# Where eight class rows run in a vision tower: a step of their own after the images, or beside images 1 and 2

## The reference, cut to what matters

```
x = _layernorm(x, gamma, beta)
x = x + gelu(x @ w1.T + b1) @ w2.T + b2          # 256 -> 1024 -> 256
h = h + _layernorm(x, gamma, beta)
m = _layernorm(h)
logits = silu(m @ rw1 + rb1) @ rw2 + rb2         # the router: 256 -> 1024 -> 8
k_logits, k_index = top_k(logits, 2); k_prob = softmax(k_logits)
for e in range(8):
    we = sum(where(k_index == e, k_prob, 0))
    out += we[:, None] * (silu(m @ w1[e] + b1[e]) @ w2[e] + b2[e])
return h + out
```

## Time and profile before

| | |
|---|---|
| median of 3 runs | 787.42 us (785.85 to 788.01) |
| the profiled execution's own time | 786.85 us |
| its span | 785.1 us |
| busy: PE / PEld / DVE / ACT / POOL | 710.4 / 624.2 / 330.0 / 296.2 / 289.0 us |
| PE busy, share of the span | 90% |
| chain that ended last | PE 72%, DVE 10%, issue 6% |

### The profile page before, as it was taken

How to read it: one execution, slowest core, us unless ns; L and a number is a source line. 1 busy time by engine, 2 the same in 40 slices (tenths; PEclk the granted TensorE clock), 3 DMA queues, 4 the chain that set the end, 5 groups by cost and what they waited for, 6 DMA issues and landing times.

```text
span 785.1 us, 15021 instructions
## 1 busy us (share of the span) xinstructions
PE 710.4 (90%) x4633; PEld 624.2 (80%) x4634; DVE 330.0 (42%) x1003; ACT 296.2 (38%) x761; POOL 289.0 (37%) x324
## 2 busy tenths in 40 slices
PE   0887999999999999999999829999999999999994
PEld 0766889988887878778876728988999899999893
DVE  5576757654424234443443461323233232333320
ACT  0433655665433335444451303333233332333321
POOL 6022866676652243445432220222232232222222
PEclk9968989999689999999998859999999999999997
DMA  9515999400000990110011324121121122112210
GB/s 222 181 23 113 287 285 288 112 0 1 1 1 1 365 333 15 41 42 28 20 35 42 136 83 143 35 34 32 34 34 34 30 34 39 24 33 34 41 20 1
DMA packets 53219, 63.92 MB, mean 81 GB/s; under 512 B 6348, under 2 KB 48768, under 8 KB 53008
## 3 DMA queue, kind: packets, MB, share of 16 engines
q1 hardware_dynamic: 43616, 53.76, 23.7%
q0 software_dynamic: 8112, 9.04, 6.8%
q10 hardware_dynamic: 1456, 0.68, 0.4%
HBM read 31.01 MB, written 31.38 MB: 79 GB/s over the span
## 4 chain that ended last, share of the span: by engine, by line
PE 72%; DVE 10%; issue 6%; DMA 3%; ACT 3%; POOL 2%; SPq 1%; POOLq 0%; DVEq 0%; ACTq 0%
PE bank L1538 68%; DMA arena<-in_L_tok_Wa 2%; POOL small L502 1%; DVE small L481 1%; ACT dense L1514 1%; DVE arena L941 1%; DMA h<-arena 1%; PE bank L1991 1%; PE bank L1855 1%; PE bank L1716 1%; POOL arena L679 1%; DVE arena L494 1%; PE bank L1570 1%; ACT arena L1436 1%; DVE dense L1173 1%
## 5 line engine op out<-in xcount | busy, mean ns | idle before, releaser
L1538 PE MATMUL bank<-arena,dense 128*128 128x256 f32 (+3 forms) x1472 | 317.6, 386 | 14.7 <-ACT dense L1514 6.0
L1538 PEld LDWEIGHTS bank<-arena,dense 128*128 128x128 f32 (+1 forms) x1472 | 256.1, 194 | 58.1 <-issue 20.5
L1514 ACT ACTIVATE dense<-bank,small 128x128 f32<-128x128 f32 x320 | 91.3, 369 | 196.8 <-PE bank L1538 196.8
L766 POOL DMA_INDIRECT out_tokens<-dense,slot_ids x40 | 77.6, 1940 | 237.7 <-DVE dense L1291 206.2
L1538 PEld LDWEIGHTS bank<-dense 128*128 128x128 f32 x1280 | 150.4, 193 | 2.0
L1538 PE MATMUL bank<-dense 128*128 128x128 f32 x1280 | 150.5, 276 | 0.0
L1538 PE MATMUL bank<-dense,arena 128*128 128x256 f32 (+2 forms) x656 | 107.7, 358 | 1.2 <-ACT arena L1378 0.7
L1538 PEld LDWEIGHTS bank<-dense,arena 128*128 128x128 f32 (+2 forms) x656 | 85.4, 193 | 19.2 <-issue 6.8
L679 POOL TENSOR_TENSOR arena<-arena 128x512 f32<-128x512 f32 x64 | 80.3, 1278 | 40.3 <-ACT arena L1398 40.3
L1538 PE MATMUL bank<-arena 128*128 128x34 f32 (+7 forms) x756 | 82.7, 304 | 1.3 <-issue 0.5
L1538 PEld LDWEIGHTS bank<-arena 128*128 128x128 f32 (+4 forms) x756 | 75.4, 179 | 9.5 <-issue 5.4
(11 more groups left out here) (213 smaller groups left out, 545.1 us busy)
## 6 DMA issues: line engine op xcount, KB each, us to landing
routed_rows<-x SPq DMA_DIRECT2D x8, 2385.0 KB, 26.1
arena<-in_L_ffn_w SPq DMA_DIRECT2D x16, 1024.0 KB
dense<-routed_rows SPq DMA_DIRECT2D x40, 132.5 KB
arena<-in_x SPq DMA_DIRECT2D x4, 512.0 KB, 7.0
arena<-in_L_attn_w SPq DMA_DIRECT2D x2, 1024.0 KB
out_tokens<-h SPq DMA_DIRECT2D x8, 256.0 KB
h<-arena SPq DMA_DIRECT2D x13, 128.0 KB
dense<-in_L_ffn_rw SPq DMA_DIRECT2D x1, 1024.0 KB, 9.5
```

Of the source, the lines that this page charges most:

```text
L766: pool.indirect_dma_start(out=sums[:, :], out_offset=bass.IndirectOffsetOnAxis(ap=slot_ids[par][:, 0:1], axis=0), in_=y[par], in_offset=No ...
L1514: act.activation(hT[par][:, k, :], psUP[par][c][:, P * m:P * m + P], ACT.Silu, bias=b1now[par][:, k:k + 1]).then_inc(hT_sb, 1)
L1538: return pe.matmul(out, lhsT, rhs, start=start, stop=stop, **kw)
```

## The change

Group 8 leaves the tail. Its work gets semaphores of its own (`c_...`), its own small buffers, and runs inside steps 1 and 2:

- Step 1: after image 2 is turned, the class rows are turned between the two tiles of `mlp_out(1)`, and their first MLP matrix (`class_hidden(w1T, ...)`) follows them.
- Step 2: `class_mlp_out` stands behind `router_out(0)`. It waits for the class rows' Gelu and for `h1_ready` to reach 2, that is the end of image 1's `finish_rows` up to its sum. Their router matrix, router output, sum and ranks stand between and behind the tiles of `mlp_out(2)`.
- DVE in step 2: `finish_rows(1)`, `finish_rows(8)`, `choose(0)`, `norm_x1(3)`, `settle(0)`, `choose(8)`, `settle(8)`; only then `finish_rows(2)` of step 3. POOL ends step 2 with `scatter(0)` and `scatter(8)` (two indirect DMAs of 8 rows).
- Step 7: `mlp_out(7)` moves ahead of the other image's router matrix (that of image 6), with `ranks(5)` between its tiles. In the tail `xm_T(7)` moves ahead of `router_sum(6)`, and `ranks(6)` stands between two halves of image 7's router matrix.

The core of the diff, PE first:

```diff
+            def class_turn(ready, src, turned_):
+                pe.wait_ge(ready, 1)
+                for k in range(KD):
+                    ins = pe.transpose(psC[:, k * B:(k + 1) * B], src[:, k * P:k * P + P], ident[0:B, 0:B])
+            def class_hidden(w, src, turned_, done):
+                pe.wait_ge(turned_, 1)
+                for m in range(KH):
+                    for k in range(KD):
+                        ins = mm(psF[0][:, m * B:(m + 1) * B], w[:, k, P * m:P * m + P], src[:, k, :],
+                                 k == 0, k == KD - 1)
+            def class_mlp_out():
+                pe.wait_ge(c_gelu_sb, 1)
+                pe.wait_ge(h1_ready, 2)
+                for k in range(KH):
+                    ins = mm(psO[0][0:B, 0:D], c_gT[:, k, :], w2T[:, k, :], k == 0, k == KH - 1)
+            def class_router_out():
+                pe.wait_ge(c_silu_sb, 1)
+                for k in range(KH):
+                    p0 = GROUP * (k % 4)
+                    ins = mm(psLT[p0:p0 + GROUP, 0:B], rw2[:, k, :], c_rT[:, k, :], k < 4, k >= 4)
+            def class_router_sum():
+                pe.wait_ge(c_lgT_sb, 1)
+                mm(psLG[0:B, 0:E], c_lgT[:, :], sel).then_inc(c_lg_ps, 1)
...
             def routing_step(g, par):
                 if not peeled or g >= 2:
+                    router_out(g - 2, par, router_use - 8)
+                if peeled and g == 2:
+                    class_mlp_out()
+                pe.wait_ge(x1T_sb, g + 1)
+                hidden(mlp_use, w1T, x1T[par], IMG)
...
+                xm_T(g - 1, 1 - par)
+                if peeled and g == B - 1:
+                    mlp_out(g, par, 0, mlp_use)
+                    ranks(g - 2)
+                    mlp_out(g, par, 1, mlp_use)
+                pe.wait_ge(xmT_sb, g)
+                hidden(router_use, rw1, xmT[1 - par], IMG)
+                if peeled and g == 2:
+                    class_turn(c_xm, c_pay[:, 0, :], c_xmT_ps)
+                if not peeled or g + 1 < B:
                     x1_T(g + 1, 1 - par)
-                if not peeled or g >= 2:
+                if not peeled or 2 <= g < B - 1:
                     ranks(g - 2)
-                if not peeled or g <= B:
-                    for j in range(1 if peeled and g == B else T):
+                if peeled and g == 1:
+                    mlp_out(g, par, 0, mlp_use)
+                    class_turn(c_xh, cx[0:B, 2, :], c_x1T_ps)
+                    mlp_out(g, par, 1, mlp_use)
+                    pe.wait_ge(m_sb, router_use + 4)
+                    class_hidden(w1T, c_x1T, c_x1T_sb, c_gelu_ps)
+                elif peeled and g == 2:
+                    pe.wait_ge(m_sb, router_use + 3)
+                    class_hidden(rw1, c_xmT, c_xmT_sb, c_silu_ps)
+                    mlp_out(g, par, 0, mlp_use)
+                    class_router_out()
+                    mlp_out(g, par, 1, mlp_use, range(0, 2))
+                    class_router_sum()
+                    mlp_out(g, par, 1, mlp_use, range(2, KH))
+                    ranks(B)
+                elif not peeled or g < B - 1:
+                    for j in range(T):
                         mlp_out(g, par, j, mlp_use)
...
-            mlp_use, use, last_use = 8 * B - 4, 8 * B, 8 * B + 4
+            use = 8 * B - 4
             router_out(B - 2, 0, 8 * (B - 1))
-            pe.wait_ge(x1T_sb, B + 1)
-            hidden(mlp_use, w1T, x1T[0], B)
-            mlp_out(B, 0, 0, mlp_use)
+            xm_T(B - 1, 1)
             router_sum(B - 2, 0)
-            xm_T(B - 1, 1)
             pe.wait_ge(xmT_sb, B)
-            hidden(use, rw1, xmT[1], IMG)
+            hidden(use, rw1, xmT[1], IMG, range(0, 2))
             ranks(B - 2)
-            xm_T(B, 0)
+            hidden(use, rw1, xmT[1], IMG, range(2, 4))
             router_out(B - 1, 1, use)
-            pe.wait_ge(xmT_sb, B + 1)
-            hidden(last_use, rw1, xmT[0], B)
             router_sum(B - 1, 1)
             ranks(B - 1)
-            router_out(B, 0, last_use)
-            router_sum(B, 0)
-            ranks(B)
```

DVE, ACT and POOL follow the same order. The parts that the prediction speaks of:

```diff
             # DVE routing_step
+                if peeled and g == 2:
+                    finish_rows(B, 0)
                 if not peeled or g >= 2:
                     choose(g - 2, par)
-                if not peeled or g + 1 <= B:
+                if not peeled or g + 1 < B:
                     norm_x1(g + 1, 1 - par)
                 if peeled and g == 1:
+                    norm_class()
                 if not peeled or g >= 2:
                     settle(g - 2, par)
+                if peeled and g == 2:
+                    choose(B, 0)
+                    settle(B, 0)
...
             finish_rows(B - 1, 1)
-            finish_rows(B, 0)
...
-            choose(B, 0)
-            settle(B, 0)
             # ACT
+            def class_hidden(done, func, bias, dst, read):
+                act.wait_ge(done, 1)
+                for m in range(KH):
+                    ins = act.activation(dst[:, m, :], psF[0][:, m * B:(m + 1) * B], func, bias=bias[:, m:m + 1])
             # POOL routing_step
                 if not peeled or g >= 2:
                     scatter(g - 2, par)
+                if peeled and g == 2:
+                    scatter(B, 0)
             # SP
-            sp.wait_ge(mlp_ps, T * B + 1)
+            sp.wait_ge(mlp_ps, T * B)
             sp.wait_ge(experts_loaded, LOW_LOADED)
             load_first(E - 2)
```

More of the change, by code:

```diff
@@ L574, in _ @@
                 store_h1(2 * it + 1, 1)
-            sp.wait_ge(h1_ready, B + 1)
+            sp.wait_ge(c_h1, 1)
             sp.dma_start(sums.rearrange("(b q) n -> b q n", b=B)[:, 0, :],
@@ L748, in _ @@
             routing_step(B - 1, 1)
[L750 to L754, removed]
+            root(pool, link, P, T, m_var, m_root, 2 * B - 1)
+            root(pool, link, P, T, m_var, m_root, 2 * B)
+            for g in (B - 2, B - 1):
                 scatter(g, g % 2)
@@ L1187, in finish_rows @@
                     dve.wait_ge(done, (g - par) * (16 * T))
-                after(dve, xmT_ps, g - 1)
-                normalize(dve, link, hrow, lambda j: rows[0:n, j, 0:D], n, tiles, m_var, m_root, 2 * g + 2
-                          ).then_inc(xm_ready, 1)
+                if not tail:
+                    after(dve, xmT_ps, g - 1)
+                normalize(dve, link, hrow, lambda j: rows[0:n, j, 0:D], n, tiles, var, root_, asked + 1
+                          ).then_inc(c_xm if tail else xm_ready, 1)
             dve.tensor_reduce(sel, ident.rearrange("p (g s) -> p s g", g=4)[:, 0:E, :], AX_X, ALU.add
@@ L1454, in _, with logits_T, gate_halves @@
                      ).then_inc(cattT_sb, 1)
-            def logits_T(g, n):
+            def logits_T(g):
                 act.wait_ge(lgT_ps, g + 1)
                 after(act, lg_ps, g)
-                act.copy(lgT[:, 0:n], psLT[:, 0:n]).then_inc(lgT_sb, 1)
-            def gate_halves(g, tiles, rows):
-                act.wait_ge(lg_gap, g + 1)
+                act.copy(lgT[:, :], psLT[:, 0:IMG]).then_inc(lgT_sb, 1)
+            def gate_halves(g):
+                tail = isinstance(g, int) and g == B
+                rows, tiles = (B, 1) if tail else (P, T)
+                gapped, count = of(g, lg_gap, c_gap)
+                act.wait_ge(gapped, count)
                 act.activation(half[0:rows, 0:tiles, :], gap[0:rows, 0:tiles, :], ACT.Tanh, scale=0.5
-                               ).then_inc(lg_half, 1)
+                               ).then_inc(c_half if tail else lg_half, 1)
             def routing_step(g, par):
@@ L1488, in _ @@
             routing_step(B - 1, 1)
-            logits_T(B - 2, IMG)
-            hidden(B, 8 * B - 4, ACT.Gelu, b1T, gT, B)
+            logits_T(B - 2)
             xm_T(B - 1, 1)
-            hidden(B - 1, 8 * B, ACT.Silu, rb1T, rT, IMG)
-            gate_halves(B - 2, T, P)
-            xm_T(B, 0)
-            logits_T(B - 1, IMG)
-            hidden(B, 8 * B + 4, ACT.Silu, rb1T, rT, B)
-            gate_halves(B - 1, T, P)
-            logits_T(B, B)
-            gate_halves(B, 1, B)
+            hidden(B - 1, 8 * B - 4, ACT.Silu, rb1T, rT, IMG, range(0, 2))
+            gate_halves(B - 2)
+            hidden(B - 1, 8 * B - 4, ACT.Silu, rb1T, rT, IMG, range(2, 4))
+            logits_T(B - 1)
+            gate_halves(B - 1)
             def rows_T(i, par):
@@ L1846, in x1_T @@
                 ins.then_inc(x1T_ps, 1)
             def xm_T(g, par):
-                tail = isinstance(g, int) and g == B
-                n, tiles = (B, 1) if tail else (P, T)
                 pe.wait_ge(xm_ready, g + 1)
-                after(pe, x1T_sb, g + 2 if not isinstance(g, int) or g + 2 <= B else B + 1)
-                for j in range(tiles):
+                after(pe, x1T_sb, g + 2 if not isinstance(g, int) or g + 2 <= B else B)
+                for j in range(T):
                     for k in range(KD):
-                        ins = pe.transpose(psT[:, k * IMG + j * P:k * IMG + j * P + n],
```

(3 more changed lines are left out.)

247 lines of the change are left out of this document (153 added, 94 removed).

## The result

| | before | after |
|---|---|---|
| median | 786.63 us (785.48 to 788.01, 4 runs) | 801.60 us (800.92 to 803.52, 4 runs) |
| ratio | | 1.0193 (95% interval 1.0167 to 1.0220) |
| profiled execution, own time / span | 786.85 / 785.1 us | 801.68 / 799.9 us |
| PE / DVE / ACT / POOL busy | 710.4 / 330.0 / 296.2 / 289.0 us | 709.3 / 330.2 / 293.5 / 289.3 us |
| span's start to step 1 | 242.4 us | 241.3 us |

The account below looks back on a forecast made before the run. PE was taken to bound the kernel where full, and the chain through the other engines where PE stands still. Terms -17.2 + 15.5 + 6.4 = +4.7 us on 786.85 gave 791.8 us, range 784.5 to 796.5.

Parts of the forecast that it names:

- What the tail gives back: Router output 5 to first expert tile: 56.7 us instead of 73.9, so 17.2 us gained.
- POOL's collision in step 7: Group 5's scatter on POOL holds the first root of finish_rows(7) back by 2.1 us.
- The landing of the last scatter: In the tail, ahead of the experts: time for the scatter to land, taken as 1.5 us, bounded by 0 and 3.
- Steps 1 to 3 without the clock: Class rows on a full PE, with late DVE in step 3: 3.85 + 8.15 + 3.5 = 15.5 us paid.
- The clock, 6.4 for four places: Clock falls at four stretches in steps 1 to 3 and the tail, 85% at 1.9 us each: 6.4 us.
- The fourth: Tail stretch from Silu wait and router output 6 through a 1.6 us stall to ACT wait: 5.1 us, a likely clock fall.
- A: Step 1's class hidden matrix, router output and stall: a 5.3 us stretch where the clock would likely fall.
- B: Step 2's class turn, turn, ranks and class hidden matrix: a 5.1 us stretch where the clock would likely fall.
- the forecast's own -1.7: Whole kernel without clock falls: 15.5 us paid in steps 1 to 3 against 17.2 gained in the tail, a small gain.
- Engine lateness does not show: Rival: no POOL collision in step 7 or DVE lateness in step 3, so 783.5 us; chance 0.16.
- The tail's work does not shrink as said: Rival: scatter's landing or last expert weight loads take 3 us more in the tail; chance 0.05.

Follow-up runs that it names:

- e1: The changed kernel with the Tanh of group 5's gates moved ahead of the Silu of image 6's router matrix in ACT's list; 792.1 us.
- e6: e5 with image 5's scatter behind both roots of finish_rows(7) in POOL's list and a buffer of their own for image 7's rows; 783.0 us.
- e3: e1 with the class rows' router output, sum and ranks put earlier among the MLP tiles of image 2; 789.9 us.
- e4: e3 with the class rows' thin router-matrix records mixed in eights between the four units of image 1's router matrix; 790.5 us.
- e5: e4 with POOL's two class scatters moved from step 2 to the tail, behind the scatter of image 6; 786.0 us.
- e7: e6 with the class rows' MLP matrix mixed into image 1's second tile, a bank part for their second matrix and their turn moved; 782.4 us.

## Why the prediction was wrong, step by step

- **The step that failed** is in "What the tail gives back": "Settle of group 5 starts at 13.8, lasts 1.94". It started at 13.5 (427.07 less 413.55) and lasted 12.6, to 439.7. The 1.94 is settle's length when the Tanh is there. The diff of PE's order was read closely, and for DVE and POOL I asked what stands ahead of each wait; for ACT I did not. Row 411.35 of the earlier trace rows was used only for the Silu's length. e1 shows the size: 9.5 us of the 9.8 that the forecast missed by, and in the tail 11.0 of the 12.6 between 56.7 and 69.3; the other 1.6 is a clock fall that the forecast had in another term.
- POOL's collision in step 7: right in place and size, once the Tanh is in place. 2.02 us of PE wait in e1 (1.6 forecast), and image 7 was turned 28.0 us after router output 5, as forecast; e6 takes the wait away.
- Tail without the Tanh: 56.7 and one fall forecast, 58.3 in e1. The landing of the last scatter, set at 1.5 within 0 to 3, is about 2.5: in the changed kernel POOL's last scatter ends at 477.7 and the row loads go out at 480.2.

```profile
480.23 1.48 SPq L637 DMA_DIRECT2D dense<-routed_rows  x2
```

From there to the first expert tile go 2.6 us (to 482.82), where the forecast took 3.39, counted from the tables. The two errors nearly cancel, 10.8 from places to experts against 10.5 forecast. That part of the agreement is luck.
- Steps 1 to 3 without the clock, 15.5: 20.7 measured, less the three falls of 1.4, 1.8 and 2.3 read from the rows above, leaves 15.2. PE's wait in step 3 was 3.24 us, 2.85 more than before against 2.9 forecast. e3 takes 1.8 of it away (settle earlier), and the class scatters on POOL were worth 1.0 from e4 to e5, against 0.7 forecast. Two sums of the forecast are 0.05 off (the terms of step 2 add up to 8.2, and 8.96 should read 8.9); nothing hangs on it.
- The clock, 6.4 for four places: all four fell, at 1.4, 1.8, 2.3 and about 2.0, together 7.5. The fourth stood behind a wait of 12.69 us here and not of 1.6; the stretch that the forecast had in mind is in e1, where the half matrix lost 1.7. That busy thin stretches keep the clock did not hold for A and B: both are busy, and where the same records stood mixed with wide ones (e4 for B, e7 for A) these falls were gone. In e7 the mixing was not the only edit. The sentence of the Trainium skill ("TensorE: Matmul & The Clock Gate", Part 1: The HAM clock gate), that the gate goes by how busy the PE has been recently, does not cover this by PE's busy share as the profile counts it: in the changed kernel PE was busy 3.82 us on end and the clock was at 1.2 GHz behind it.
- That the sum's sign came from the clock was wrong for the changed kernel: by the forecast's own -1.7 and the Tanh's 9.5 it would have been slower without any fall. For e1 it fits: 5.0 us over the kernel before, with falls of about 7 in its rows. No run shows e1 without the falls and otherwise the same, so this is argued.
- "Engine lateness does not show" (0.16) did not come: both waits were there, 3.24 us in step 3 and, with the Tanh in place, 2.02 in the tail.
- "The tail's work does not shrink as said" stood at 0.05 with 3 us. Its title fits what came, its mechanism does not: it spoke of the scatter's landing and the weight loads. No rival named an instruction in ACT's list.

## What to carry to other kernels

When work is reordered on one engine, lay the new order beside the list of every other engine, and look for small instructions that now stand behind work that comes later: a 0.2 us Tanh behind a moved block cost 9.5 us here. Work moved to where PE is full cost its length here, and in addition what it made late on the engines that serve the next step; in e5 and e6 it paid to put scatters in POOL's list behind the small answers that someone waited for. Mixing thin matmuls with wide ones instead of issuing them in a run is worth a try: the rows of e4 and e7 show the fall behind the run gone, but the medians of neither show a gain. And read an edit's price from its own stretch, when stages ahead of it move by more than the edit does.

## What the runs showed of the hardware that was not expected

- The same 32 thin records (8 columns) cost their 3.6 us and nothing else when mixed in eights with 256-column ones (e4: 10.67 us for 64 records), and 1.4 to 1.8 us more behind them when issued in one run (changed kernel).
- Waits of 0.63 us (e5) and 1.42 us (e3) in step 3 kept 2.4 GHz, one of 1.66 us (e4) did not. In the tail the same wait of 2.02 us came four times and the clock fell each time, but not at the same place: in e1 and e5 the turn behind it took 0.66 us and the half matrix 5.41, in e3 and e4 the turn took 1.1 and the half matrix 5.7. What decides the place, and whether 1.42 always holds, stays open.
- An indirect DMA of 8 rows held POOL for 0.86 us (e4), one of 128 rows for 0.96 us (e1): the few rows saved almost nothing there.
